# A fused attention and feed-forward layer on one core: one projection unit of each even slot stands between the two halves of a tile's logits

## What is computed

```python
xn = _layernorm(x)
qkv = jnp.einsum('bsd,ed->bse', xn, Wqkv).reshape(B, S, 3 * H, D)     # B 1, S 2048, H 16, D 128
q, k, v = qkv[:, :, :H], qkv[:, :, H:2 * H], qkv[:, :, 2 * H:]
logits = jnp.einsum('bqhd,bkhd->bhqk', q, k) * D ** (-0.5)
w = jax.nn.softmax(logits, axis=-1)
out = jnp.einsum('bhqk,bkhd->bqhd', w, v).reshape(B, S, H * D)
attn = jnp.einsum('bse,de->bsd', out, Wout)
ffn = _bitlinear(jax.nn.sigmoid(_bitlinear(xn, w1)) * _bitlinear(xn, w2), w3)
return x + attn + ffn
```

## Time and profile before

| | |
|---|---|
| median of 3 executions | 1875.28 us (1875.22 to 1876.1) |
| the profiled execution, its own time | 1874.88 us |
| span of its profile | 1873.1 us |
| granted TensorE clock, mean | 0.999 |
| TensorE (PE) busy | 1846.1 us, 99% of the span |
| weight loads (PEld) busy | 1657.9 us, 89% |
| DVE busy | 1592.8 us, 85% |
| POOL busy | 1342.0 us, 72% |
| ACT busy | 1259.9 us, 67% |

### The profile page before, as it was taken

One profiled execution on the slowest core, in us unless ns is written; L12 is line 12 of the kernel. 1 busy time (PEld: TensorE's weight loads), 2 busy tenths in 40 slices (PEclk: granted clock), 3 DMA queues, 4 the chain that ended last, 5 costly groups with the idle time before them and its releaser, 6 DMA issues.

```text
span 1873.1 us, 33365 instructions
## 1 busy us (share of the span) xinstructions
PE 1846.1 (99%) x11556; PEld 1657.9 (89%) x11556; DVE 1592.8 (85%) x2095; ACT 1259.9 (67%) x1714; POOL 1342.0 (72%) x508
## 2 busy tenths in 40 slices
PE   6989999999999999999999999999999999999999
PEld 5879889899998989899889998899898998899988
DVE  7488888888988888888889888888888888889885
ACT  6466666766667676666767676676766667676675
POOL 2457686877768687776868768687876868777685
PEclk9999999999999999999999999999999999999999
DMA  3057776776767777676776767677676767767675
GB/s 121 1 138 172 163 174 159 175 169 155 174 157 174 164 165 175 151 179 162 162 181 150 176 160 168 162 163 182 155 170 160 169 161 173 171 154 170 158 170 136
DMA packets 195928, 298.74 MB, mean 159 GB/s; under 512 B 37920, under 2 KB 57120, under 8 KB 195872
## 3 DMA queue, kind: packets, MB, share of 16 engines
q1 hardware_dynamic: 195872, 298.08, 68.0%
HBM read 12.71 MB, written 2.10 MB: 8 GB/s over the span
## 4 chain that ended last, share of the span: by engine, by line
PE 83%; issue 6%; POOL 4%; SPq 3%; DVE 3%; ACT 1%; DMA 1%; POOLq 0%; DVEq 0%; ACTq 0%
PE ps_o L416 33%; PE ps_s L407 11%; PE ps_s L408 11%; PE ps_s L409 11%; PE ps_t L395 4%; PE ps_t L385 4%; PE ps_s L376 4%; SPq L317 3%; POOL parts L1200 3%; PE ps_o L425 1%; PE ps_o L427 1%; PE ps_o L426 1%; POOL hid_lo L1187 1%; DVE prob L1056 1%; DVE row_max L1046 1%
## 5 line engine op out<-in xcount | busy, mean ns | idle before, releaser
L1200 POOL TENSOR_TENSOR parts<-raw,parts 128x2048 fp32r<-128x2048 f32 x254 | 1175.4, 4628 | 432.7 <-ACT parts L791 432.3
L803 ACT ACTIVATE prob<-ps_s,neg_max 128x1024 f32<-128x1024 f32 x512 | 567.0, 1114 | 434.1 <-DVE neg_max L1050 433.8
L1046 DVE TENSOR_REDUCE row_max<-ps_s 128x1 f32<-128x1024 f32 x512 | 612.4, 1212 | 106.0 <-PE ps_s L409 86.6
L1056 DVE STREAM_TRANSPOSE prob<-prob 128x1024 f32<-128x1024 f32 x508 | 599.7, 1218 | 56.2 <-ACT prob L803 55.6
L791 ACT CAST parts<-raw 128x2048 fp32r<-128x2048 f32 x254 | 486.2, 1914 | 105.8 <-DMA raw<-prob 105.7
L416 PE MATMUL ps_o<-parts,v_hi 128*128 128x256 f32 x4064 | 516.2, 280 | 0.6 <-POOL v_lo L1193 0.6
L416 PEld LDWEIGHTS ps_o<-parts,v_hi 128*128 128x128 f32 x4064 | 498.8, 189 | 15.6 <-POOL v_lo L1193 5.3
L407 PE MATMUL ps_s<-k_hi,q_hi 128*128 128x512 f32 x1024 | 400.5, 391 | 6.7 <-ACT prob L803 6.2
L408 PE MATMUL ps_s<-k_lo,q_hi 128*128 128x512 f32 x1024 | 399.6, 390 | 0.0
L409 PE MATMUL ps_s<-k_hi,q_lo 128*128 128x512 f32 x1024 | 399.5, 390 | 0.0
L416 PE MATMUL ps_o<-parts,v_lo 128*128 128x256 f32 x2032 | 275.8, 278 | 0.0
(11 more groups left out here) (135 smaller groups left out, 1543.9 us busy)
## 6 DMA issues: line engine op xcount, KB each, us to landing
raw<-prob SPq DMA_DIRECT2D x2032, 128.0 KB, 2.4
v_raw<-v_turned SPq DMA_DIRECT2D x244, 64.0 KB, 2.0
w_raw<-wqkv_dram SPq DMA_DIRECT2D x32, 128.0 KB, 2.5
y<-x_dram SPq DMA_DIRECT2D x4, 512.0 KB, 4.8
wo_raw<-wqkv_dram SPq DMA_DIRECT2D x16, 128.0 KB, 2.5
wo_raw<-wo_dram SPq DMA_DIRECT2D x16, 128.0 KB, 2.3
out_dram<-y SPq DMA_DIRECT2D x7, 256.0 KB, 3.2
w_raw<-w_dram SPq DMA_DIRECT2D x2, 704.0 KB, 7.7
```

The lines of the kernel that those rows point to most:

```text
L803: nc.scalar.activation(tile, logit, ACT.Exp, bias=neg_max[:, t:t + 1], scale=SCALE, accum_out=row_sum[:, t, half:half + 1]).then_inc(s_exp, 1)
L1046: nc.vector.reduce_max(row_max[:, t, half:half + 1], ps_s[:, 2 * half:2 * half + 2, :].rearrange("p b n -> p (b n)"), AX_X).then_inc(s_mx, 1)
L1056: nc.vector.transpose(tile, tile).then_inc(s_xp, 1)
L1200: nc.gpsimd.tensor_tensor(half_of(0, half), moved(p, half), half_of(1, half), ALU.subtract).then_inc(s_pl, 1)
```

## The change

In heads 1 to 15 the unit of an even slot is issued between the two halves of the logits, with the waits that belong to it, in place of behind the products. The order becomes: logits half 0, unit, logits half 1, products. The unit of t = 6 keeps its place. Head 0 keeps its order, and odd slots keep theirs. The code of the slot is moved into four functions; instructions and waits are the same in number and kind on every engine.

```diff
+            def second_half_products(h, t, first, final):
+                if t == 6 and not final:
+                    pe.wait_ge(s_wsp[2], count(1, h, 2))
+                    pe.wait_ge(s_qlo, count(4, h, 2))
+                    values(ps_v[0], 0)
+                if t >= 6:
+                    product_step(h, (t - 6) // 2, 1, first)
+                elif not first:
+                    product_step(before(h), 5 + t // 2, 1)
+
+            def projections(h, t, first, final):
...
+                elif t == 0:
+                    pe.wait_ge(s_vt, count(4, h, 2))
+                    values(ps_v[1], 3)
...
+                if t == 2:
...
+                    pe.wait_ge(s_vt, count(4, h, 3))
+                    queries(ps_v[0], 1)
+                if t == 4:
+                    pe.wait_ge(s_vt, count(4, h, 4))
+                    queries(ps_v[1], 2)
+                if t == 8:
+                    pe.wait_ge(s_qlo, count(4, h, 3))
+                    queries(ps_v[1], 3)
+                if not final:
+                    if t == 10:
+                        pe.wait_ge(s_vt, count(4, h, 4 + 1))
+                        values(ps_v[0], 1)
+                    if t == 12:
+                        pe.wait_ge(s_wsp[0], count(1, h, 2))
+                        pe.wait_ge(s_qlo, count(4, h, 4))
+                        queries(ps_v[1], 0)
+                    if t == 14:
+                        pe.wait_ge(s_vt, count(4, h, 4 + 2))
+                        values(ps_v[0], 2)
...
                         if t:
                             pe.wait_ge(s_exp, count(32, h, 2 * (t - 1) + half + 1))
                         logits(t, half, None if t else h)
+
+                        if half == 0 and not first:
+                            if t % 2 == 0:
+                                projections(h, t, first, final)
                     if t % 2:
...
+                        outputs(h, t, first)
+                        first_half_products(h, t, first)
+                        projections(h, t, first, final)
                     else:
...
+                        second_half_products(h, t, first, final)
                         if first:
...
+                            projections(h, t, first, final)
```

More of the change, by code:

```diff
@@ L554, in output_step, with outputs, first_half_products @@
                 out_projection(ps_y, o_hi, o_lo, s_y)
+            def outputs(h, t, first):
+                if t >= 7:
+                    output_step(h, (t - 7) // 2)
+                elif not first:
+                    output_step(before(h), 5 + t // 2)
+            def first_half_products(h, t, first):
+                if t >= 5:
+                    product_step(h, (t - 5) // 2, 0, first)
+                elif not first:
+                    product_step(before(h), 6 + t // 2, 0)
+            def second_half_products(h, t, first, final):
[5 more added lines that the diff above has]
+                    product_step(h, (t - 6) // 2, 1, first)
+                elif not first:
+                    product_step(before(h), 5 + t // 2, 1)
@@ new lines, in projections @@
+            def projections(h, t, first, final):
+                if t == 0 and first:
+                    values(ps_v[0], 2)
+                    values(ps_v[1], 3)
+                elif t == 0:
+                    pe.wait_ge(s_vt, count(4, h, 2))
+                    values(ps_v[1], 3)
+                if t == 1 and first:
+                    ffn_down_last(0, range(3, FB))
+                    ffn_down_last(1, range(FB))
+                if t == 3 and first:
+                    ffn_down_last(3, range(FB))
+                if t == 2:
+                    if first:
+                        ffn_down_last(2, range(FB))
+                    pe.wait_ge(s_vt, count(4, h, 3))
[16 more added lines that the diff above has]
+                        pe.wait_ge(s_vt, count(4, h, 4 + 2))
+                        values(ps_v[0], 2)
@@ L565, in head @@
                         logits(t, half, None if t else h)
+                        if half == 0 and not first:
+                            if t % 2 == 0:
+                                projections(h, t, first, final)
                     if t % 2:
[L567 to L574, removed]
-                    else:
[L576 to L583, removed]
@@ L586, in head @@
[L586 to L596, removed]
@@ L597, in head @@
-                    if t == 2:
-                        if first:
[L599 to L618, removed]
+                        outputs(h, t, first)
```

## The result

The changed kernel takes **1900.4 us** (median of 4 executions, 1899.93 to 1901.07) against 1875.43 us before: ratio 1.0135, 95% interval 1.0123 to 1.0147. The forecast was 1900.0 us.

The account below looks back on a forecast made before the run. TensorE, busy 99% of the span, was taken as the bound. Stalls of +29.6 us less 4.5 us coming back gave +25.1 us on 1874.88 us (0.40 below the median): 1900.0 us, 8-in-10 range 1885 to 1919.

Parts of the forecast that it names:

- The bound and the chain: TensorE bounds; behind its work must fit the 3.19 us from second-half logits through maximum, neg_max and exponential to next logits.
- 102 x (0.14 + 0.15) = 29.6 us: Each of 102 moved even slots waits 0.14 us for the exponential and loses 0.15 us in the logits behind it.
- the estimate of 2.62: Products by the skill page's issue-gap formula: 2.62 us instead of 2.82, wait 0.34 us, total about +45 us; set aside.
- Only one maximum exposed: Moved slots: DVE's first maximum ends before the second half's logits do, leaving one exposed, so the chain stays 3.19 us.
- Nothing in the odd slots: Odd slots: 3.68 us of cover is half a microsecond over the chain, so no loss; output step and products take 3.45 us.
- 4.5 us come back: Slots 5 to 7: TensorE's waits for POOL's v_lo and wo_lo shrink; half of 8.6 us taken, -4.5 us.
- The moved waits: Moved units' own waits are on work of an earlier slot, closest w_sp for t = 12; no cost counted.
- The rule on weight loads: Skill page: the queue pulls weight loads ahead of matmuls in flight; if past the wait too, only the wait is paid.
- The rival built on it: Moved slots: only the wait is paid, 102 x 0.14 = 14.3 us, less 4.5: 1884.7 us; chance 0.05.
- The other rivals: Even slots: cover suffices, 1866 at best, about 1871 us, chance 0.04; or longer chain, 1917 or 1936 us, together 0.12.
- ACT is free too: Moved slots: ACT's DMA-waiting cast ends 4.66 us behind the odd slot's start, before ACT is wanted at some 5.7 us.
- Keys to keys 112.4: One head, from keys to keys, should take about 112.4 us: 110.60 + 7 x 0.29 - 0.3.

Follow-up runs that it names:

- experiment 1: Changed kernel with five of the unit's six matmuls between the logits halves and the sixth behind the products, in all 102 moved slots: 1880.14 us, ratio 1.0026.
- experiment 2: Changed kernel with the unit placed behind both halves of the logits and ahead of the products: 1875.56 us, ratio 1.0000 to the kernel before.
- experiment 5: Changed kernel with four of the unit's matmuls between the logits halves and two behind the products: 1876.01 us, ratio 1.0002 to the kernel before.
- experiment 6: Changed kernel with the second half's maximum in even slots over 512 instead of 1024 columns: 1875.17 us, ratio 0.9998 to the kernel before.
- The late half: Changed kernel with only the units of t = 8, 10, 12 and 14 between the halves (57 slots): 1891.17 us, ratio 1.0082 to the kernel before.
- experiment 9: Kernel before, with the values unit of t = 6 moved to t = 5 and four queries matmuls of t = 8 moved to t = 6: 1875.01 us, ratio 0.9996.
- the early half: Changed kernel with only the units of t = 0, 2 and 4 between the halves (45 slots): 1884.55 us, ratio 1.0046 to the kernel before.
- experiment 11: Kernel before, with the values unit of t = 6 moved to t = 5 and two queries matmuls of t = 8 moved to t = 6: 1871.26 us, ratio 0.9980.
- experiment 3: Changed kernel with one product matmul repeated once in each of the 102 moved slots, 12.0 us of added work: 1900.64 us.
- Experiment 4: Changed kernel with one product matmul repeated twice in each of the 102 moved slots, 24.1 us of added work: 1900.23 us.

## Why the prediction was right, point by point

- **The bound and the chain.** Shown. Only the work behind the last logits matmul, against 3.19 us, decides: experiments 1, 2 and 5 change the work, experiment 6 the chain, and each takes away all or most of the loss.
- **102 x (0.14 + 0.15) = 29.6 us.** The late half gives 0.275 a slot over 57 slots. In the head shown above, slot 10 has 0.15 of wait and 0.14 of restart; the products' 2.82 us of the row was right, since the estimate of 2.62 would have made the wait 0.34. One slot was mis-sized: the exponential of slot 0 comes 0.08 us later than in the others, and L409 to L407 is 3.27 us (989.27 to 992.54) where I took 3.19 for all. It is so in the 13 heads of the hardware loop, and 3.19 in heads 14 and 15; over 13 slots that is 1.0 us. These are the chain's two records on TensorE in slot 0:

```profile
989.27 0.39 PE L409 MATMUL ps_s<-k_hi,q_lo 128*128 128x512 f32 x1
...
992.54 0.50 PE L407 MATMUL ps_s<-k_hi,q_hi 128*128 128x512 f32 x1
```

- **Only one maximum exposed.** Shown by the rows of DVE above. In slot 8 L409 to L407 is 3.19 us in the changed kernel; with both halves back to back and little behind the products it is 3.66 (experiment 9).
- **Nothing in the odd slots.** Right: 3.45 us for the output step and its products.
- **4.5 us come back.** That the size fits is luck: I took half of the bound of 8.6 us and had no row for the half. From the first logits matmul of a slot to that of the next, mean of heads 1 to 14, slot 5 takes 6.41 us before and 6.32 after, although 0.13 of restart has come into it; slot 6 takes 6.95 and 6.88, slot 7 6.30 and 6.24. That gives back 0.35 us a head, 5.0 us in all; the early half agrees (about 4.8). The wait at t = 5 is gone, as I had said, and the loss at t = 7 is about halved: an unstalled odd slot takes 6.17.
- **The moved waits.** No wait of a unit shows in the table of TensorE's waits.
- **The rule on weight loads.** The Trainium skill ("TensorE: Matmul & The Clock Gate", section "Step-by-step: what each phase is for") lets the queue pull weight loads ahead of matmuls in flight. The trace bears that out where nothing waits, and not past a wait: before, the weight load of L407 comes 0.11 us ahead of its matmul behind products, and in the changed kernel both start at 1059.20. The rival built on it, 1884.7 us, is out: 1900.4 was measured, and each wait is followed by its restart.
- **The other rivals.** The cover did not suffice. That case had about 1871 us; experiment 6 lets the cover suffice and takes 1875.2, with the waits for v_lo as before (5.2 us in 21). The chain was as short as its bare length in all moved slots but slot 0 and one more: by the starts, TensorE waits 0.14 us in the moved slots and 0.22 in slot 0. The one more is in head 1. In its slot 10 ACT stood 4.07 us for a DMA and had its cast and a second one to finish, while neg_max was ready at 270.89 (270.68 + 0.21). TensorE waited 1.08 us there:
```profile
269.75 1.91 ACT L809 CAST parts<-raw 128x2048 fp32r<-128x2048 f32 x1 [4.07 <-DMA raw<-prob]
271.56 0.40 ACT L698 CAST w_sp<-w_raw 128x256 fp32r<-128x256 f32 x1
271.87 1.11 ACT L821 ACTIVATE prob<-ps_s,neg_max 128x1024 f32<-128x1024 f32 x1
```

  In the kernel before the same DMA was waited for 2.90 us, and the unit covered it. My step "ACT is free too" holds in all slots but this one, and the price is 0.9 us, once. Why that DMA came later was not tried.
- **Keys to keys 112.4.** Measured 112.3, which is also what its own sum gives (110.60 + 2.03 - 0.3 = 112.33). Two more figures were a little off, and nothing rests on them: a slot like slot 10 loses 0.46 + 0.15 = 0.61 us and not 0.60, and the upper end of the range, 1919, is 2 us above the 1917 that it is said to stand for.

The errors are slot 0 (1.0 us too little), the one late DMA (0.9 too little), the size of a slot's loss (0.275 against 0.29, 1.5 too much over 102 slots) and what came back (0.5 more than taken). They cancel almost wholly. That the sum fits to 0.4 us is luck to that extent; the mechanism and each term's size to about a microsecond and a half are not.

## What to carry to other kernels

On a saturated engine a reordering is judged by one subtraction: the work between the instruction that starts a chain on other engines and the one that waits for its end, less the length of that chain, taken from a place in the trace where it lies bare. Leave a margin, since TensorE loses its pace before any wait is visible: here 0.10 us over the chain was not enough, and 0.31 was. Work that nobody waits for is worth most when it is cut in pieces and each is spent where it covers something, as experiment 11 does with one unit: two matmuls in one slot, four in another.

## What I had not expected

- **A wait of 0.02 us costs as much restart as one of 0.46.** Behind a late exponential, L407 to L408 is 0.33 to 0.34 us in slot 10 of the last head before (0.46 us of wait), in the changed kernel (0.15) and in experiment 3 (0.02).
- **There is a loss with no wait at all.** In experiment 1 the logits wait for an exponential in slot 0 at most, and yet a head takes 0.3 us longer than before (110.88 from 970.44 to 1081.32). The weight load behind the semaphore comes 0.09 instead of 0.22 us ahead, and behind slot 0 with its matmul. Over 15 heads that is about the 4.5 us.

```profile
970.44 5.46 PE ps_s L376 x24
1081.32 5.46 PE ps_s L376 x24
```

- **204 matmuls more at no cost.** Experiment 4 adds 24 us of matmuls to an engine that is 98% busy, and the time stays within 0.2 us of the changed kernel without them.
- Why ACT starts the exponential of slot 0 later after neg_max (0.12 us instead of 0.04) was not tried and stays open. It is not the change: the kernel before has the same delay there. It is not the length of ACT's idle time either: in head 8 ACT was idle for 5.08 us (neg_max ends at 991.16, the exponential starts at 991.28), in head 14 for 5.00 us (1664.80 and 1664.84). The late starts in slot 0 are those of heads 1 to 13, the hardware loop; heads 14 and 15, written out, have none.
